# Interleaving projection pieces with transposes, and moving the context transposes last, in the attention stage of an eight-stage kernel

## The chip, the cores and the metric

The kernel runs on one core of a Trainium2 chip. The metric is the device time of one execution in microseconds; before the change the median of three executions is 2313.64 us (2311.55 to 2314.72).

## What is computed

The reference chains four attention layers and four feed-forward layers of different kinds on `x` (2 batches, 1024 rows, 256 features) with a context of 77 rows per batch. The change lies in the seventh link, called stage 6 in the kernel (stages count from 0), which is the last attention layer. Cut to what matters:

```
def _L3_xattn_ref(x, latents, mask, ...):      # x = context (77 rows), latents = layernormed rows (1024)
    xn = layer_norm(x, g_x, b_x)
    ln = layer_norm(latents, g_l, b_l)
    q = ln @ Wq
    kv_in = concatenate([xn, ln], axis=1)      # 77 + 1024 = 1101 keys
    k, v = split(kv_in @ Wkv)                  # 16 heads of 64
    sim = (q * 64 ** -0.5) @ k.T
    attn = softmax(where(mask, sim, max_neg))
    out = (attn @ v) @ Wout
    return layer_norm(out, g_o, b_o)
```

Everything is float32. Scores are computed with queries on the partitions, so that the softmax runs along the free axis; the probabilities must then be transposed before they can be multiplied with `v`.

## The kernel before

The program is written engine by engine: each engine has its own function `stage6` with its instructions in the order in which it will run them, and semaphores between them. Nothing is reordered by a scheduler.

**Units.** The 16 heads are taken in pairs, 8 pairs for each of 2 batches, so there are 16 pairs `n`, and a pair has 8 tiles of 128 queries. The loop runs over units `u`; in unit `u` TensorE (PE) computes the scores of tile `u = 8n + qt`, and transposes the probabilities of tile `u - 1`. There are 128 such tiles. In what follows the parts of a unit on PE are called

- *scores* (`scores`): the product with the context keys of both heads (2 x 77 columns), then with the 1024 other keys of each head, all from line 614, the helper for matmuls;
- *p0, p1, p2, p3* (`p_turn`, L1177): four transposes of 128 x 128 each; p0 and p1 are head 0 of the pair, p2 and p3 head 1. One group fills one PSUM bank;
- *c* (`ctx_turn`, L1184 and L1185): the two transposes of the 77 context keys;
- *r* (`sums_turn`, L1192): in even units, two transposes of the reciprocal sums of the softmax of a pair of tiles;
- *w0, w1* (`piece`): in even units, two pieces of the q, k and v projections for the next head pair. Which pieces come is set by `u % 8`: in 0 both halves of q (512 columns each), in 2 the first two blocks of v with the context keys, and 512 columns of k, in 4 and 6 shorter ones;
- *v* (`weigh`): in odd units, the product of the transposed probabilities of two tiles with v;
- *o* (`project`): the output projection, in units 60 to 66 and in those after 123, even ones only.

**The ring.** The results of p, c, r, w, v and o all go to a ring of three PSUM banks. `r6_no` numbers them in the order of the table, and

```
        def r6_bank(key):
            return 5 + r6_no[key] % 3
                def free_bank(key):
                    t = r6_no[key]
                    if t >= 3:
                        copied(pe, r6_keys[t - 3])
                    return r6_bank(key)
```

So before PE writes entry `t` it waits until entry `t - 3` has been copied out. ScalarE (ACT) copies p0 and p1 (L1727), w0 (L1696 for q; L1698, L1704 and L1705 for v and the context keys) and r (L1745). VectorE (DVE) copies w1 (L2401 for q, L2402 for k), c (L2482), p2 and p3 (L2485), and v (L2477, with the multiplication by the reciprocal sums).

**Softmax.** DVE finds the maxima of the two heads (L2463 over 1024 columns, L2464 joins the context's maximum and releases ACT). ACT then does the exponential of head 0 and of head 1 (L1738, 1101 columns each, followed by a read of the accumulated sum). On ACT a unit is: copy p0, copy p1, exponential of head 0, copy w0 (even units), exponential of head 1, copy r (even units). On DVE it is: the reciprocal sums (even units), the maxima, copy w1, or v in odd units, copy c, copy p2, copy p3.

The order in the table before is, for an even unit, p0, p1, w0, w1, c, p2, p3, r, and o where there is one; for an odd unit p0, p1, v, c, p2, p3.

Of the kernel before, what the change touches and what calls it, by code (L numbers as in the profile page):

```python
# [16 lines left out]
P = 128  # L17
# [6 lines left out]
C = 77  # L24
# [27 lines left out]
def build(nc, A, out, stages=ALL_STAGES):  # L52

    ctx = ExitStack()
    with ctx:
# [316 lines left out]
        NU = 128  # L372
        N7 = {77 + 4 * t: t for t in range(8)}
        r6_no, r6_sb, done = {}, {}, {"act": 0, "dve": 0}
        for u in range(NU + 5):
            even = u % 2 == 0
            turn = 1 <= u <= NU
            batch = [("p", u - 1, 0), ("p", u - 1, 1)] if turn else []
            if even and u // 8 < 15:
                batch += [("w", u // 8 + 1, u % 8), ("w", u // 8 + 1, u % 8 + 1)]  # L380
            if not even and 3 <= u < NU + 3:
                batch += [("v", (u - 3) // 2)]
            batch += [("c", u - 1), ("p", u - 1, 2), ("p", u - 1, 3)] if turn else []
            if even and 2 <= u <= NU:
                batch += [("r", (u - 2) // 2)]
            if even and u >= 4 and (u // 2 - 2) % 32 >= 28:
                batch += [("o", u // 2 - 2)]
            if u in N7:
                batch += [("n", N7[u])]
            for key in batch:  # L390
                act_copies = key[0] == "r" or key[0] == "p" and key[2] < 2 or key[0] == "w" and key[2] % 2 == 0
                eng = "act" if act_copies else "dve"
                done[eng] += 1
                r6_no[key] = len(r6_no)
                r6_sb[key] = (r6_act if act_copies else r6_dve, done[eng])
# [216 lines left out]
        def _(pe):  # L612
# [506 lines left out]
            def stage6():  # L1119
# [75 lines left out]
                def weigh(g):  # L1195

                    n = g // 4
                    copied(pe, ("p", 2 * g + 1, 1))
                    copied(pe, ("p", 2 * g + 1, 3))
                    bank = free_bank(("v", g))  # L1200
                    for i in range(NKT):
                        rows = P if i < NKT - 1 else C
                        for h in range(2):
                            r = 64 * h
                            last = mm(PS[r:r + 64, bank, 0:2 * P], s6_v[n % 2][0:rows, i, r:r + 64], s6_pt[g % 2][h][0:rows, i], start=(i == 0), stop=(i == NKT - 1))
                    last.then_inc(r6_mm, 1)
# [13 lines left out]
                for u in range(NU + 5):  # L1220
# [4 lines left out]
                    if u == 0:  # L1225
                        pe.wait_ge(ln_xa, 8 * half_no[6] + 8)
                        turn6(2, 0, 5)
                        turn6(3, 0, 6)
                        turn6(2, 1, 7)
                        pe.wait_ge(ln_fa, 4 * tr + 3)  # L1230
                        turn6(3, 1, 5)
                        pe.wait_ge(ln_fa, 4 * tr + 4)
                        pe.wait_ge(ln_fv, 4 * tr + 4)
                    if 1 <= u <= NU:
                        p_turn(u - 1, 0)
                        p_turn(u - 1, 1)
# [138 lines left out]
        def _(act):  # L1375
# [309 lines left out]
            def stage6():  # L1685
# [27 lines left out]
                for j in range(0, 8, 2):  # L1713
# [2 lines left out]
                            act.activation(XN[:, t, :], X[:, t, :], ACT.Identity, bias=ln_bias[:, t:t + 1], scale=lnrs[:, t:t + 1]).then_inc(ln_xa, 1)  # L1716
                    act.wait_ge(c6_mm, j + 1)
                    piece(0, j, j).then_inc(c6_sb, 1)
                for u in range(NU + 5):
                    even = u % 2 == 0  # L1720
                    n, j = u // 8 + 1, u % 8
                    if 1 <= u <= NU:
                        v = u - 1
                        g, c0 = v // 2, (v % 2) * P
                        for i in range(2):
                            bank = filled(("p", v, i))
                            act.activation(s6_pt[g % 2][0][:, 4 * i:4 * i + 4, c0:c0 + P], PS[:, bank, :].rearrange("p (a n) -> p a n", a=4), ACT.Copy).then_inc(r6_act, 1)  # L1727
                    if u < NU:
                        g = u // 2
                        if u == 0:  # L1730
# [5 lines left out]
                        for h in range(2):  # L1736
# [2 lines left out]
                                           accum_out=s6_sm[:, g % 2, 2 * (u % 2) + h:2 * (u % 2) + h + 1]).then_inc(a6_p, 1)  # L1739
                            if h == 0 and even and n < 16:  # L1740
                                piece(n, j, filled(("w", n, j))).then_inc(r6_act, 1)
                    if even and 2 <= u <= NU:
                        g = (u - 2) // 2
                        bank = filled(("r", g))
                        act.activation(s6_r[g % 2], PS[:, bank, 0:2 * P], ACT.Copy).then_inc(r6_act, 1)  # L1745
# [106 lines left out]
        def _(dve):  # L1852
# [533 lines left out]
            def stage6():  # L2386
# [17 lines left out]
                def filled(key):  # L2404

                    dve.wait_ge(r6_mm, r6_no[key] + 1)
                    return r6_bank(key)

                def normed(g):

                    t = 8 * (g // 32) + 2 * (g % 4)
# [34 lines left out]
                for u in range(NU + 6):  # L2446
# [31 lines left out]
                    if 1 <= u <= NU:  # L2478
                        v = u - 1
                        g, c0 = v // 2, (v % 2) * P  # L2480
                        bank = filled(("c", v))
                        dve.tensor_copy(s6_ptc[g % 2][:, :, c0:c0 + P], PS[0:C, bank, 0:2 * P].rearrange("p (h n) -> p h n", h=2)).then_inc(r6_dve, 1)  # L2482
                        for i in (2, 3):
                            bank = filled(("p", v, i))
                            dve.tensor_copy(s6_pt[g % 2][1][:, 4 * (i - 2):4 * (i - 2) + 4, c0:c0 + P], PS[:, bank, :].rearrange("p (a n) -> p a n", a=4)).then_inc(r6_dve, 1)  # L2485
                    if even and u >= 4 and (u // 2 - 2) % 32 >= 28:
                        normed(u // 2 - 2)
                    if u in N7:
# [170 lines left out]
```

## Time and profile before

| what | value |
|---|---|
| median of three executions | 2313.64 us (2311.55 to 2314.72) |
| the profiled execution | 2314.89 us |
| its span | 2313.1 us |
| PE busy | 2136.5 us, 92% of the span |
| DVE busy | 1397.3 us, 60% |
| ACT busy | 1027.7 us, 44% |
| stage 6 (first unit's scores to about the last transposes) | 1108 to 2196 us of the span, some 47% of it |

The profiled execution took 1.8 us more than its span, which begins with its first recorded instruction, and lies 1.25 us above the median. The busy time of PE is modelled from the starts of matmuls, which are pipelined: a transpose counts 0.27 us as busy, while in an undisturbed group one starts every 0.11 us. A short wait of PE therefore shows only partly as idle time, and is best read from the starts of neighbouring groups.

### The profile page before, as it was taken

The page shows a single profiled execution, that of the slowest core. Times are in us where ns is not written, and L with a number is a line of the kernel's source. Part 1 is how long each engine was busy: PE and PEld are TensorE (multiplying, and loading weights), DVE is VectorE, ACT ScalarE, POOL GpSimd, SP SyncE. Part 2 cuts the span into 40 slices and gives each one's busy share as a digit, 9 for nine tenths or more (in the row PEclk, how much of TensorE's full clock was granted, in tenths as well). Part 3 has the DMA queues.
Part 4 walks back from the last instruction along what each step waited for, and adds up shares of the span by engine and source line. Part 5 has one row for each costly group of instructions (what it writes and reads, how often), then busy time and mean ns, then how long its engine had stood idle before and what let it go on. Part 6 is the DMA issues. An engine that isn't in the chain of part 4 may idle for free.

```text
span 2313.1 us, 34544 instructions
## 1 busy us (share of the span) xinstructions
PE 2136.5 (92%) x13157; PEld 1517.1 (66%) x13157; DVE 1397.3 (60%) x3066; ACT 1027.7 (44%) x2143; POOL 129.4 (6%) x122
## 2 busy tenths in 40 slices
PE   6996997868999799796999999999999999999998
PEld 4874996434999678555566666666666666666653
DVE  5763112672444678687566666666666767677555
ACT  5652442530121522487445444454445444454445
POOL 1002111005122000000100000000000000000000
PEclk9997999889999999898999999999999999999999
DMA  3605897024797600200000000000000000000001
GB/s 116 175 3 169 306 328 237 19 77 135 258 324 267 199 1 1 78 1 7 5 1 1 1 1 1 1 1 1 1 1 1 1 1 1 1 1 1 1 1 37
DMA packets 109263, 159.78 MB, mean 69 GB/s; under 512 B 12555, under 2 KB 85165, under 8 KB 109101
## 3 DMA queue, kind: packets, MB, share of 16 engines
q1 hardware_dynamic: 101805, 134.80, 17.6%
q0 software_dynamic: 7296, 22.78, 2.9%
q8 instruction: 107, 1.75, 0.3%
q14 instruction: 55, 0.45, 0.1%
HBM read 127.64 MB, written 29.91 MB: 68 GB/s over the span
## 4 chain that ended last, share of the span: by engine, by line
PE 51%; DVE 4%; ACT 2%; issue 1%; ACTq 0%; DVEq 0%
PE ps L614 38%; PE ps L1177 10%; PE ps L1184 1%; ACT w_odd L1738 1%; PE ps L1192 1%; DVE small L2463 1%; PE ps L1080 0%; DVE arena L2485 0%; DVE arena L2402 0%; PE ps L1185 0%; DVE w_odd L2401 0%; DVE small L2348 0%; ACT xn_tok L1599 0%; PE ps L1089 0%; ACT out_feat L1656 0%
## 5 line engine op out<-in xcount | busy, mean ns | idle before, releaser
L614 PE MATMUL ps<-arena,w_odd 128*128 128x128 f32 (+4 forms) x2352 | 436.9, 439 | 3.0 <-DVE arena L2140 1.2
L614 PE MATMUL ps<-arena 128*64 128x256 f32 (+4 forms) x3216 | 388.4, 371 | 8.1 <-DVE arena L2271 4.3
L2463 DVE TENSOR_REDUCE small<-ps 128x1 f32<-128x1024 f32 x256 | 312.6, 1221 | 81.7 <-PE ps L614 81.5
L1727 ACT ACTIVATE arena<-ps 128x512 f32<-128x512 f32 x256 | 139.2, 595 | 452.0 <-PE ps L1177 451.9
L614 PEld LDWEIGHTS ps<-arena 128*64 128x64 f32 (+4 forms) x3216 | 254.2, 154 | 120.1 <-issue 22.4
L614 PEld LDWEIGHTS ps<-arena,w_odd 128*128 128x128 f32 (+3 forms) x2352 | 245.2, 187 | 105.1 <-issue 99.8
L1738 ACT ACTIVATE w_odd<-ps,small 128x1101 f32<-128x1101 f32 x256 | 302.8, 1183 | 9.7 <-DVE small L2464 7.3
L1177 PEld LDWEIGHTS ps<-ident,w_odd 128*128 128x128 f32 x2048 | 223.1, 141 | 123.4 <-issue 110.4
L1177 PE MATMUL ps<-ident,w_odd 128*128 128x128 f32 x2048 | 281.3, 277 | 12.0 <-DVE w_odd L2401 2.9
L2485 DVE COPY arena<-ps 128x512 f32<-128x512 f32 x256 | 164.3, 683 | 5.4 <-PE ps L1177 3.1
L614 PE MATMUL ps<-xn_feat,w_even 128*128 128x512 f32 (+1 forms) x352 | 137.9, 523 | 5.1 <-DVE xn_feat L2384 2.3
L1528 ACT ACTIVATE arena<-ps,arena 128x128 f32<-128x128 f32 x184 | 67.5, 368 | 92.9 <-PE ps L614 82.2
L614 PE MATMUL ps<-arena,w_even 128*128 128x256 f32 (+2 forms) x608 | 107.8, 330 | 0.5 <-DVE x_res L1921 0.5
L614 PE MATMUL ps<-xn_feat,w_odd 128*128 128x512 f32 x224 | 103.4, 602 | 0.0
L614 PE MATMUL ps<-w_odd,arena 128*128 128x256 f32 (+1 forms) x436 | 101.5, 379 | 0.0
L614 PEld LDWEIGHTS ps<-arena,w_even 128*128 128x128 f32 x608 | 94.8, 192 | 8.6 <-DVE x_res L1921 0.6
L614 PE MATMUL ps<-w_even,xn_feat 128*128 128x128 f32 (+1 forms) x576 | 96.2, 313 | 0.0
L1548 ACT ACTIVATE arena<-ps 128x128 f32<-128x128 f32 (+1 forms) x117 | 32.4, 277 | 141.2 <-PE ps L614 140.6
L614 PEld LDWEIGHTS ps<-xn_feat,w_even 128*128 128x128 f32 x352 | 62.2, 192 | 45.1 <-issue 38.9
L2161 DVE TENSOR_SCALAR arena<-ps,arena 128x256 f32<-128x256 f32 x62 | 30.0, 484 | 96.8 <-PE ps L614 96.8
L614 PEld LDWEIGHTS ps<-w_odd,arena 128*128 128x128 f32 (+1 forms) x436 | 79.5, 190 | 9.0
L614 PEld LDWEIGHTS ps<-w_even,xn_feat 128*128 128x128 f32 x576 | 73.7, 192 | 17.1 <-issue 16.8
(395 smaller groups left out, 2930.8 us busy)
## 6 DMA issues: line engine op xcount, KB each, us to landing
w_odd<-in_s_w SPq DMA_DIRECT2D x32, 1024.0 KB
w_odd<-in_s_wgu SPq DMA_DIRECT2D x30, 704.0 KB
w_even<-in_s_w SPq DMA_DIRECT2D x15, 1024.0 KB
arena<-expert_rows_in SPq DMA_DIRECT2D x62, 130.0 KB
w_odd<-in_s_wd SPq DMA_DIRECT2D x30, 256.0 KB
out_feat<-in_s_wgu SPq DMA_DIRECT2D x10, 704.0 KB, 4.2
expert_rows_in<-zero_row POOLq DMA_DIRECT2D x1, 5070.0 KB, 32.4
vo_rows<-w_odd SPq DMA_DIRECT2D x8, 616.0 KB
```

The costliest lines, as they stand in the source:

```text
L614: return pe.matmul(o, lhsT, rhs, start=start, stop=stop, **kw)
L1177: last = pe.transpose(PS[:, bank, j * P:(j + 1) * P], src[:, c0:c0 + P], ident[:, :])
L1184: pe.transpose(PS[0:C, bank, 0:P], s6_p[u % 2][0][:, S:KV], ident[:, :])
L1192: last = pe.transpose(PS[:, bank, i * P:(i + 1) * P], s6_rb[g % 2][:, 2 * i:2 * i + 2].rearrange("p h d -> p (h d)"), ident[:, :])
L1528: act.activation(s1_h[q][:, m], PS[:, (M * i + m) % 4, 0:TS], ACT.Gelu, bias=s1_bt[w][:, m:m + 1]).then_inc(per["mu_act", 1], 1)
L1548: act.activation(s3_s[0:rows, u % 2, 0:TS], PS[0:rows, u % 4, 0:TS], ACT.Silu).then_inc(per["mu_act", 3], 1)
L1727: act.activation(s6_pt[g % 2][0][:, 4 * i:4 * i + 4, c0:c0 + P], PS[:, bank, :].rearrange("p (a n) -> p a n", a=4), ACT.Copy).then_inc(r6_ ...
L1738: act.activation(s6_p[u % 2][h][:, 0:KV], s6_sc[h], ACT.Exp, bias=s6_nm[:, u % 2, h:h + 1], accum_out=s6_sm[:, g % 2, 2 * (u % 2) + h:2 * ...
L2161: dve.tensor_scalar(mx_y[st][v % 2][:, j], PS[:, 4 + n % 2, 0:D], es_xg[:, v, 1:2], None, ALU.mult).then_inc(per["md_sb", st], 1)
L2463: link(dve.tensor_reduce(m, s6_main[h], AX.X, ALU.max, negate=True))
L2485: dve.tensor_copy(s6_pt[g % 2][1][:, 4 * (i - 2):4 * (i - 2) + 4, c0:c0 + P], PS[:, bank, :].rearrange("p (a n) -> p a n", a=4)).then_inc( ...
```

## The change

In units `u` with `1 <= u < 120` and `u % 8` of 0 or 2 (29 units, called *long* here) the ring's order becomes p0, w0, p1, w1, r, p2, p3, c, then o. PE follows this order. ACT copies p1 no longer before the exponential of head 0 but after the copy of w0, that is ahead of the exponential of head 1. DVE copies c after p3. All other units stay as they are. `weigh` gets one more wait, for the copy of c, since that is no longer implied by the copy of p3.

```
+        def long_pieces(u):
+
+            return 1 <= u < 120 and u % 8 in (0, 2)
+
         for u in range(NU + 5):
             even = u % 2 == 0
             turn = 1 <= u <= NU
+            if long_pieces(u):
+                pieces = [("w", u // 8 + 1, u % 8 + i) for i in range(2)]
+                batch = [("p", u - 1, 0), pieces[0], ("p", u - 1, 1), pieces[1], ("r", (u - 2) // 2)]
+                batch += [("p", u - 1, 2), ("p", u - 1, 3), ("c", u - 1)]
+                if u >= 4 and (u // 2 - 2) % 32 >= 28:
+                    batch += [("o", u // 2 - 2)]
...
                     copied(pe, ("p", 2 * g + 1, 1))
                     copied(pe, ("p", 2 * g + 1, 3))
+                    copied(pe, ("c", 2 * g + 1))
...
+                    if long_pieces(u):
+                        p_turn(u - 1, 0)
+                        piece(n, j, free_bank(("w", n, j))).then_inc(r6_mm, 1)
+                        p_turn(u - 1, 1)
+                        piece(n, j + 1, free_bank(("w", n, j + 1))).then_inc(r6_mm, 1)
+                        sums_turn((u - 2) // 2)
+                        p_turn(u - 1, 2)
+                        p_turn(u - 1, 3)
+                        ctx_turn(u - 1)
+                        if u >= 4 and (u // 2 - 2) % 32 >= 28:
+                            project(u // 2 - 2)
+                        continue
...
-                        for i in range(2):
-                            bank = filled(("p", v, i))
-                            act.activation(s6_pt[g % 2][0][:, 4 * i:4 * i + 4, c0:c0 + P], PS[:, bank, :].rearrange("p (a n) -> p a n", a=4), ACT.Copy).then_inc(r6_act, 1)
+                        for i in range(1 if long_pieces(u) else 2):
+                            p_copy(v, i)
...
                             if h == 0 and even and n < 16:
                                 piece(n, j, filled(("w", n, j))).then_inc(r6_act, 1)
+                            if h == 0 and long_pieces(u):
+                                p_copy(u - 1, 1)
...
-                        bank = filled(("c", v))
-                        dve.tensor_copy(s6_ptc[g % 2][:, :, c0:c0 + P], PS[0:C, bank, 0:2 * P].rearrange("p (h n) -> p h n", h=2)).then_inc(r6_dve, 1)
+                        if not long_pieces(u):
+                            context_copy(v)
                         for i in (2, 3):
                             bank = filled(("p", v, i))
                             dve.tensor_copy(s6_pt[g % 2][1][:, 4 * (i - 2):4 * (i - 2) + 4, c0:c0 + P], PS[:, bank, :].rearrange("p (a n) -> p a n", a=4)).then_inc(r6_dve, 1)
+                        if long_pieces(u):
+                            context_copy(v)
```

**PE, a unit with `u % 8 == 2`, from piece w1 to the unit's end, before.** L614 is w1 (`w_even` holds the k weights here), L1184 and L1185 are c, L1177 first p2, then p3 (`w_odd` holds the probabilities), L1192 is r. `r6_act` and `r6_dve` are the waits for copies by ACT and by DVE.

```order
L614 MATMUL ps<-xn_feat,w_even 128x512 [waits r6_act]
L614 MATMUL ps<-xn_feat,w_even 128x512
L1184 MATMUL ps<-ident,w_odd 77x128 [waits r6_act,a6_p]
L1185 MATMUL ps<-ident,w_odd 77x128
L1177 MATMUL ps<-ident,w_odd 128x128 [waits r6_act,a6_p]
L1177 MATMUL ps<-ident,w_odd 128x128 x3
L1177 MATMUL ps<-ident,w_odd 128x128 [waits r6_dve,a6_p]
L1177 MATMUL ps<-ident,w_odd 128x128 x3
L1192 MATMUL ps<-ident,arena 128x128 [waits r6_dve,a6_rb]
L1192 MATMUL ps<-ident,arena 128x128
```

The same stretch after the change; 18 lines were added ahead of it, so that L632, L1195, L1202, L1203 and L1210 are what L614, L1177, L1184, L1185 and L1192 were.

```order
L632 MATMUL ps<-xn_feat,w_even 128x512 [waits r6_act]
L632 MATMUL ps<-xn_feat,w_even 128x512
L1210 MATMUL ps<-ident,arena 128x128 [waits r6_act,a6_rb]
L1210 MATMUL ps<-ident,arena 128x128
L1195 MATMUL ps<-ident,w_odd 128x128 [waits r6_act,a6_p]
L1195 MATMUL ps<-ident,w_odd 128x128 x3
L1195 MATMUL ps<-ident,w_odd 128x128 [waits r6_dve,a6_p]
L1195 MATMUL ps<-ident,w_odd 128x128 x3
L1202 MATMUL ps<-ident,w_odd 77x128 [waits r6_act,a6_p]
L1203 MATMUL ps<-ident,w_odd 77x128
```

Between w1 and p3 there are six transposes in both. r and c have changed places, and the last group of the unit now waits for ACT (the copy of r) where it waited for DVE (the copy of c).

**ACT, the same unit, before.** L1727 copies p0 and p1, L1738 is an exponential, L1698, L1704 and L1705 copy w0, L1745 copies r.

```order
L1727 ACTIVATE arena<-ps 128x4x128 [waits r6_mm] x2
L1738 ACTIVATE w_odd,small<-ps,small 128x1101 [waits a6_mx,r6_mm]
L1698 ACTIVATE arena<-ps 128x256 [waits r6_mm]
L1704 ACTIVATE w_even<-ps 64x77
L1705 ACTIVATE w_even<-ps 64x77
L1738 ACTIVATE w_odd,small<-ps,small 128x1101 [waits a6_mx]
L1745 ACTIVATE arena<-ps 128x256 [waits r6_mm]
```

The same unit after the change (L1754, L1773, L1729, L1735, L1736 and L1782 for L1727, L1738, L1698, L1704, L1705 and L1745):

```order
L1754 ACTIVATE arena<-ps 128x4x128 [waits r6_mm]
L1773 ACTIVATE w_odd,small<-ps,small 128x1101 [waits a6_mx,r6_mm]
L1729 ACTIVATE arena<-ps 128x256 [waits r6_mm]
L1735 ACTIVATE w_even<-ps 64x77
L1736 ACTIVATE w_even<-ps 64x77
L1754 ACTIVATE arena<-ps 128x4x128 [waits r6_mm]
L1773 ACTIVATE w_odd,small<-ps,small 128x1101 [waits a6_mx]
L1782 ACTIVATE arena<-ps 128x256 [waits r6_mm]
```

One copy of 128 x 512 has moved from ahead of the first exponential to ahead of the second, so that it stands between the first exponential and the copy of r.

## Rows read from the trace of the kernel before

**Rows 1.** The page: busy us, share of the span, instructions, by engine.

```profile
PE 2136.5 (92%) x13157; PEld 1517.1 (66%) x13157; DVE 1397.3 (60%) x3066; ACT 1027.7 (44%) x2143; POOL 129.4 (6%) x122
```

**Rows 2.** Windows of the span, us: busy time by engine, then PEclk, DMA share, GB/s.

```profile
1108.50:2195.00 1086.50, 1063.44 (x7094) 703.53 (x7095) 731.18 (x1498) 521.32 (x960) 2.98 (x1) 1.00 0.00 1
...
1127.10:1132.00 4.90, 4.90 (x18) 2.70 (x19) 2.59 (x8) 0.42 (x1) 0.00 (x0) 0.65 0.01 3
```

**Rows 3.** Waits in stage 6: us in total, times, longest us.

```profile
PE ps L1177 <- DVE w_odd L2401: 2.9, 13, 0.2
PE ps L1177 <- DVE arena L2402: 2.9, 13, 0.2
```

**Rows 4.** Timeline of unit 18, PE: start us, us, then [idle before].

```profile
1264.23 0.27 PE L1184 MATMUL ps<-ident,w_odd 128*77 128x128 f32 x1
...
1264.45 0.60 PE L1177 MATMUL ps<-ident,w_odd 128*128 128x128 f32 x4
1265.27 0.63 PE L1177 MATMUL ps<-ident,w_odd 128*128 128x128 f32 x4 [0.22 <-DVE arena L2402]
1265.73 0.38 PE L1192 MATMUL ps<-ident,arena 128*128 128x128 f32 x2
1265.95 0.43 PE L614 MATMUL ps<-w_even,w_odd 128*128 128x154 f32 x2
```

**Rows 5.** Timeline of unit 18, DVE.

```profile
1261.62 0.16 DVE L2464 TENSOR_TENSOR small<-small 128x1 f32<-128x1 f32 x1
...
1264.43 0.69 DVE L2402 COPY arena<-ps 128x512 f32<-128x512 f32 x1 [1.33 <-PE ps L614]
```

**Rows 6.** Timeline of unit 18, ACT.

```profile
1260.94 1.09 ACT L1727 ACTIVATE arena<-ps 128x512 f32<-128x512 f32 x2 [5.02 <-PE ps L1177]
1261.91 1.18 ACT L1738 ACTIVATE w_odd<-ps,small 128x1101 f32<-128x1101 f32 x1
...
1263.07 0.39 ACT L1698 ACTIVATE arena<-ps 128x256 f32<-128x256 f32 x1
...
1263.57 0.23 ACT L1705 ACTIVATE w_even<-ps 64x77 f32<-64x77 f32 x1
1263.82 1.18 ACT L1738 ACTIVATE w_odd<-ps,small 128x1101 f32<-128x1101 f32 x1
...
1266.15 0.39 ACT L1745 ACTIVATE arena<-ps 128x256 f32<-128x256 f32 x1 [1.06 <-PE ps L1192]
```

**Rows 7.** Timeline of unit 64, which also has a projection: DVE, ACT and PE.

```profile
1650.18 0.16 DVE L2464 TENSOR_TENSOR small<-small 128x1 f32<-128x1 f32 x1
...
1650.43 1.18 ACT L1738 ACTIVATE w_odd<-ps,small 128x1101 f32<-128x1101 f32 x1 [1.61 <-DVE small L2464]
...
1651.61 0.59 ACT L1696 ACTIVATE w_odd<-ps 128x512 f32<-128x512 f32 x1
...
1652.34 1.07 PE L1177 MATMUL ps<-ident,w_odd 128*128 128x128 f32 x8 [0.54 <-ACT w_odd L1696]
...
1653.84 1.97 PE L614 MATMUL ps<-w_even,xn_tok 128*128 128x256 f32 x8 [0.22 <-DVE arena L2485]
```

**Rows 8.** Timeline of unit 16, ACT and PE.

```profile
1245.06 1.19 ACT L1738 ACTIVATE w_odd<-ps,small 128x1101 f32<-128x1101 f32 x1
...
1246.73 1.18 ACT L1738 ACTIVATE w_odd<-ps,small 128x1101 f32<-128x1101 f32 x1
...
1249.26 0.38 PE L1192 MATMUL ps<-ident,arena 128*128 128x128 f32 x2
```

**Rows 9.** Timeline of unit 66: first exponential, and start of the projection.

```profile
1674.97 1.18 ACT L1738 ACTIVATE w_odd<-ps,small 128x1101 f32<-128x1101 f32 x1 [1.60 <-DVE small L2464]
...
1678.51 0.67 PE L614 MATMUL ps<-w_even,xn_tok 128*128 128x256 f32 x2 [0.22 <-DVE arena L2485]
```

**Rows 10.** Timeline of unit 74: first exponential, and start of the next unit.

```profile
1748.87 1.18 ACT L1738 ACTIVATE w_odd<-ps,small 128x1101 f32<-128x1101 f32 x1
...
1752.12 0.53 PE L614 MATMUL ps<-w_even,w_odd 128*128 128x154 f32 x2
```

More of the change, by code:

```diff
@@ L377, in build @@
             turn = 1 <= u <= NU
+            if long_pieces(u):
[4 more added lines that the diff above has]
+                    batch += [("o", u // 2 - 2)]
+                for key in batch:
+                    act_copies = key[0] == "r" or key[0] == "p" and key[2] < 2 or key[0] == "w" and key[2] % 2 == 0
+                    eng = "act" if act_copies else "dve"
+                    done[eng] += 1
+                    r6_no[key] = len(r6_no)
+                    r6_sb[key] = (r6_act if act_copies else r6_dve, done[eng])
+                continue
             batch = [("p", u - 1, 0), ("p", u - 1, 1)] if turn else []
@@ L1233, in stage6 @@
                         pe.wait_ge(ln_fv, 4 * tr + 4)
+                    if long_pieces(u):
[9 more added lines that the diff above has]
+                            project(u // 2 - 2)
+                        continue
                     if 1 <= u <= NU:
@@ L1718, in stage6, with p_copy @@
                     piece(0, j, j).then_inc(c6_sb, 1)
+                def p_copy(v, i):
+                    g, c0 = v // 2, (v % 2) * P
+                    bank = filled(("p", v, i))
+                    act.activation(s6_pt[g % 2][0][:, 4 * i:4 * i + 4, c0:c0 + P], PS[:, bank, :].rearrange("p (a n) -> p a n", a=4), ACT.Copy).then_inc(r6_act, 1)
                 for u in range(NU + 5):
@@ L1723, in stage6 @@
                         v = u - 1
-                        g, c0 = v // 2, (v % 2) * P
-                        for i in range(2):
-                            bank = filled(("p", v, i))
-                            act.activation(s6_pt[g % 2][0][:, 4 * i:4 * i + 4, c0:c0 + P], PS[:, bank, :].rearrange("p (a n) -> p a n", a=4), ACT.Copy).then_inc(r6_act, 1)
+                        for i in range(1 if long_pieces(u) else 2):
+                            p_copy(v, i)
                     if u < NU:
@@ L2407, in filled, with context_copy @@
                     return r6_bank(key)
+                def context_copy(v):
+                    g, c0 = v // 2, (v % 2) * P
+                    bank = filled(("c", v))
+                    dve.tensor_copy(s6_ptc[g % 2][:, :, c0:c0 + P], PS[0:C, bank, 0:2 * P].rearrange("p (h n) -> p h n", h=2)).then_inc(r6_dve, 1)
                 def normed(g):
```

## The prediction

> **What bounds the kernel now.** I read the page first. PE is busy for 2136.5 us of the span, DVE and ACT far less [rows 1]. The windows then give stage 6: 1063.44 of 1086.50 us PE-busy at a granted clock of 1.00 throughout [rows 2]. So PE sets the pace of the stage, and the change can only act through the moments at which PE waits inside a unit, or through waits that it adds. It adds and removes no arithmetic.
>
> The waits of PE in the stage show two groups that belong to the long units: transposes of L1177 wait 13 times for the copy of w1 by L2401 and 13 times for that by L2402 [rows 3]. The times look tiny, 2.9 us each, since a transpose's busy time is longer than its slot. The timeline shows the real size. In unit 18 (`u % 8` is 2) the group p2 starts at 1264.45 and p3 at 1265.27, 0.82 us later, while a slot is 0.11 us (the two of c fill 1264.23 to 1264.45) and four of them are 0.44 us [rows 4]. The wait is thus 0.38 us, and it ends with DVE's copy of w1, which runs from 1264.43 to 1265.12 [rows 5]. This wait, in 26 ordinary long units and in a different form in three others, is what a reordering of the ring could win: 26 x 0.38 = 9.9 us.
>
> **Part one: the wait ahead of p3.** Count the ring before: w0, w1, c, p2, p3; three entries ahead of p3 stands w1. After: w1, r, p2, p3; three ahead of p3 stands w1 again. Between the end of w1 on PE and the start of p3 lie two short transposes (c before, r after) and the four of p2, six slots either way: w1 ends where c starts, at 1264.23, and p3 could start at 1264.89 in both orders. What precedes w1 is the same work too (p0, p1, w0, in another order), so w1 ends at the same time, DVE starts its copy at the same time, and p3 waits for it until 1265.27 as before. Gain: 0. The move of p1 behind w0, and of c's copy behind those of p2 and p3 on DVE, does not touch this: c's copy stood behind w1's before as well.
>
> **Part two: the new wait of c.** Three entries ahead of c now stands r, and r is copied by ACT after the exponential of head 1. Before, r's neighbour waited for c's copy, which DVE had long made. So I follow ACT through unit 18:
>
> - First exponential. In the trace it starts at 1261.91, two copies after 1260.94, so a copy takes 0.485 us from start to start [rows 6]. With p1's copy moved away it waits only for DVE's maximum, ready at 1261.62 + 0.16 = 1261.78 [rows 5]. From such an end to an exponential that was waiting for it takes 0.09 us (1650.34 to 1650.43) [rows 7]. Start: 1261.87.
> - Copy of w0 starts 1.16 us later and holds ACT for 0.75 us (1263.07 to 1263.82) [rows 6]: 1263.03, and free at 1263.78.
> - Copy of p1, 0.485 us: the second exponential starts at 1264.27, where it started at 1263.82.
> - Copy of r: 1.16 us after it, 1265.43; it takes 0.39 us [rows 6], to 1265.82.
> - PE starts 0.14 us after the end of a copy by ACT (1651.61 + 0.59 = 1652.20, against 1652.34) [rows 7]: c can start at 1265.96.
>
> PE reaches c when p3 has been issued, at 1265.73, where r started before [rows 4]. It waits 0.23 us, and a group that restarts after a wait takes some 0.02 us more (p3: 0.46 for 0.44). The unit ends 0.25 us later. The odd unit behind it has no waits of the ring on PE in which this could be recovered: the stage is bound by PE, and a delay moves all that follows. Twelve units are of this kind (10, 18, ..., 114 but not 66 and 74): **+3.0 us**. Unit 2 runs its scores at the lower of the two clocks (0.65 in that window [rows 2]), so that the copies of p0 and p1 come late there, and moving one away frees the exponential; I count 0, at most 0.25.
>
> In units with `u % 8` of 0, w0 is a half of q: two exponentials are 1.67 us apart [rows 8], and w1 and w0 are both long on PE. From 1245.06: second exponential at 1245.06 + 1.67 + 0.485 = 1247.22, copy of r at 1248.38, its end at 1248.77, c free at 1248.91. PE gets there at 1249.26 [rows 8]. There are 0.35 us to spare: **0** for 13 units.
>
> Three long units have a late first exponential; there PE already waits for ACT's copy of w0 ahead of p2. After the change the row on ACT is w0, p1, exponential, r, and c waits at its end. From the first exponential to the start of c is 1.16 + 0.75 + 0.485 + 1.16 + 0.39 + 0.14 = 4.09 us, and 0.25 us for c itself. Unit 66: 1674.97 + 4.34 = 1679.31, where the projection started at 1678.51 [rows 9]: +0.80. Unit 74: 1748.87 + 4.34 = 1753.21 against 1752.12 [rows 10]: +1.09 at most, since its exponential may start a little earlier. Unit 64, with q for w0 (1.67 in place of 1.16 + 0.75): 1650.43 + 4.10 = 1654.53 against 1653.84 [rows 7]: +0.69. Together **+2.6 us**.
>
> **Part three, what costs nothing.** The second exponential ends 0.45 us later; the next unit's scores wait for it, but 1264.27 + 1.18 + 0.2 for the read of the sum is 1265.65, and those scores come at 1266.2. p1's copy now ends at 1264.38; p2, three entries behind, could start at 1264.45 and is held to 1264.52, which is hidden by p3's wait to 1265.27. r waits for w0's copy, done by 1263.8. `weigh` now waits for c's copy, which is DVE's third behind w1's (p2, p3, c); c is issued by 1266.2 and copied by about 1267, while `weigh` comes behind the next unit's scores and two groups, 3.2 us of work (4.9 x 0.65 [rows 2]). If that cover went, the product with v would be late. No DMA moves, and no instruction is added.
>
> **Sum.** 3.0 + 2.6 = +5.6 us on the profiled execution, 2314.89 to 2320.5. That execution lies 1.25 above the median, so the median goes from 2313.64 to **2319.2 us**, 0.24% slower.
>
> A rule to weigh against the rows: two copies take 0.485 us from start to start here [rows 6]. The Trainium skill (page "ScalarE: Activation LUTs", section "What ACT_TABLE_LOAD costs") gives 186 ns plus 0.833 ns per column for an activation with immediate operands, less 93 ns where two overlap; for 512 columns that is an estimate of 0.52 us, and the trace does not quite agree. By that page each of the 15 waits would be 0.035 us longer, and the sum 6.1 us.
>
> **Bounds of the unknown.** No row shows c waiting for r. From below it is 0 per unit, if ACT catches up; the three odd units alone then give +2.6. From above it is what the row of ACT gives if nothing overlaps: a copy at its full 0.60 us instead of 0.485, and both exponentials followed by their read, 1.39 instead of 1.16: 0.58 us more, 0.83 in all. I take 0.25, since every interval in it is one that ACT shows in this order of operations.
>
> **Rivals.** A change of 0.2% (4.6 us) is about what a measurement of this kernel can tell from none.
>
> - *ACT is in time.* Should PE come to c some 0.2 us later than I read, or ACT run ahead, the regular units cost nothing: 2313.64 + 2.6 = 2316.2. For it speaks that the margin is small; against it that the trace repeats its units to within hundredths.
> - *The wait ahead of p3 goes, and c doesn't wait.* If w1's copy did not decide (if, say, the release of p3 hung on ACT's copy of w0 or on the order of DVE's copies), alternating pieces and groups would win the 0.38 us in 26 units: 2313.64 - 9.9 = 2303.7. It decides only if c's wait is absent too, for p3's relief alone would bring PE to c earlier, to stand there for ACT. Against it: rows 3 name the copies of w1 in just 26 cases, and the count of the ring leaves w1 where it was. That the change doesn't do what it is for belongs here: the ring after is a new order with the same distance.
> - *The late case for ACT.* The chain on ACT is 0.45 us longer than I think, and the units of the other kind, with 0.35 to spare, wait too: 12 x 0.70 + 13 x 0.10 + 2.6 + 3 x 0.45 = 13.7 us, 2327.3.
> - *The clock.* In the window from 1127.10, behind a wait of PE, the clock was 0.65 [rows 2]. Fifteen more short waits could lower it. The scores and first groups there took 4.9 us, at full clock 0.65 of it, 3.2 us; 15 x 1.7 = 25 us, 2339. Against it: 26 waits of 0.38 us leave it at 1.00 in rows 2. The Trainium skill ("TensorE: Matmul & The Clock Gate", section "A second HAM failure mode: psum-queue depth-cycling") tells of a kernel that cycled through PSUM banks with short idle times of PE and whose clock kept switching between its two levels; that rule speaks against a change that adds a wait to a ring, but the trace of this ring so far doesn't agree with it.
>
> **How the numbers follow.** Forecast 0.62; ACT in time 0.21; faster 0.06; late ACT 0.08; clock 0.03. Of the forecast's 0.62 I give 0.07 to ends under 4.6 us, as a sum of 5.6 with an error of 0.1 us per unit may have. Faster 0.06, within 0.28, slower 0.66. The range goes from 2315.0 (ACT in time, less 1 us for the spread of the runs) to 2324.0 (the regular wait at 0.6 instead of 0.25): it leaves out the faster case, the clock and most of the late case.
>
> **What would show it.** In the profile after, p3 still starts 0.82 us after p2 in long units; the copy of r starts before c and right behind the second exponential; c in units with `u % 8` of 2 is released by ACT, 0.2 to 0.3 us after p3's last slot; and in the waits of PE the context transposes (L1202, before L1184) appear as held by the copy of r (L1782, before L1745) 12 to 15 times. Units with `u % 8` of 0 keep their length. The prediction is wrong if p3 starts 0.44 us after p2, or if c follows p3 without a gap.

## The result and the profile after

| | before | after |
|---|---|---|
| median of five executions | 2313.64 us (2311.22 to 2316.34) | 2321.69 us (2320.03 to 2326.81) |
| profiled execution | 2314.89 us, span 2313.1 | 2320.03 us, span 2318.3 |

The ratio is 1.0041, with a 95% interval of 1.0029 to 1.0053: 6.7 to 12.3 us slower. The forecast was 5.6 us and a time of 2319.2 in a range of 2315.0 to 2324.0. The direction and the range were right, and the size came out too small. The profiled execution alone shows +5.1 us, but beside what the change does to the waits, two things of about equal size and opposite sign stand in the difference of these two profiles; the experiments below find both.

The page of the changed kernel. Its first line holds something that the prediction had denied: 64 instructions more than the 34544 of before.

```profile
span 2318.3 us, 34608 instructions
## 1 busy us (share of the span) xinstructions
PE 2139.7 (92%) x13157; PEld 1513.7 (65%) x13157; DVE 1401.5 (60%) x3066; ACT 1026.3 (44%) x2143; POOL 129.4 (6%) x122
```

Against [rows 1] nothing has changed in the work. Now the timeline of unit 18 after the change, which answers to [rows 4 to 6]. First the loads of weights (PEld), since they part p2 from p3: L1210 is r, L1195 p2 and then p3, L1202 and L1203 are c, L632 the scores of unit 19. The columns are start us, us, and in brackets the idle time before and what ended it.

```profile
1262.71 0.14 PEld L1210 LDWEIGHTS ps<-ident,arena 128*128 128x128 f32 x1 [0.17 <-issue]
1263.02 0.42 PEld L1195 LDWEIGHTS ps<-ident,w_odd 128*128 128x128 f32 x4 [0.17 <-issue]
1263.71 0.42 PEld L1195 LDWEIGHTS ps<-ident,w_odd 128*128 128x128 f32 x4 [0.28 <-issue]
1264.45 0.14 PEld L1202 LDWEIGHTS ps<-ident,w_odd 128*77 128x77 f32 x1 [0.32 <-ACT w_odd L1773]
```

The same on PE itself, where the two groups are merged in one row:

```profile
1262.71 0.38 PE L1210 MATMUL ps<-ident,arena 128*128 128x128 f32 x2
1263.05 1.32 PE L1195 MATMUL ps<-ident,w_odd 128*128 128x128 f32 x8
1264.48 0.30 PE L1202 MATMUL ps<-ident,w_odd 128*77 128x128 f32 x1
1264.62 0.27 PE L1203 MATMUL ps<-ident,w_odd 128*77 128x128 f32 x1
1264.73 0.43 PE L632 MATMUL ps<-w_even,w_odd 128*128 128x154 f32 x2
```

And ACT: L1773 are the two exponentials, L1729 to L1736 the copy of w0, L1754 that of p1, L1782 that of r.

```profile
1260.39 1.18 ACT L1773 ACTIVATE w_odd<-ps,small 128x1101 f32<-128x1101 f32 x1 [0.34 <-DVE small L2507]
...
1261.56 0.38 ACT L1729 ACTIVATE arena<-ps 128x256 f32<-128x256 f32 x1
...
1262.31 0.60 ACT L1754 ACTIVATE arena<-ps 128x512 f32<-128x512 f32 x1
1262.80 1.18 ACT L1773 ACTIVATE w_odd<-ps,small 128x1101 f32<-128x1101 f32 x1
...
1263.95 0.38 ACT L1782 ACTIVATE arena<-ps 128x256 f32<-128x256 f32 x1
```

The chain stands as forecast: 4.09 us from the first exponential (1260.39) to c (1264.48), with 1.17, 0.75, 0.49, 1.15, 0.38 and 0.15 for its steps. p3 still waits for w1's copy: from the end of w1, where r starts (1262.71), to p3 it is 1.0 us (1263.71 for its weights), as in [rows 4] from 1264.23 to 1265.27. Behind p3 PE now stands until r has been copied: p3's four transposes begin by 1264.10, one more slot of 0.11 us would be 1264.21, and c begins at 1264.48, 0.27 us later. The row of L1202 above names the second exponential (L1773) as what ended the wait, but that was done at 1263.98; the copy of r ended at 1264.33, and it is the only other one that c waits for. In unit 18 the wait is too short to show as idle time of PE. It does so in three units, and there the copy of r is named:

```profile
PE ps L1202 <- ACT arena L1782: 1.1, 3, 0.4
```

The clearest reading is the length of each unit, from the start of its scores to that of the next one's. Where the clock is the same it repeats to some 0.01 us. "Before, again" and "after, again" are second profiles, from the experiments; the first of them comes from another chip.

| unit | before | before, again | after | after, again |
|---|---|---|---|---|
| `u % 8` of 0 (median) | 8.36 | 8.36 | 8.37 | 8.36 |
| `u % 8` of 2 (median) | 7.99 | 7.99 | 8.25 | 8.25 |
| 2 | 9.72 | 8.09 | 8.35 | 8.35 |
| 64 | 16.05 | 16.04 | 16.64 | 16.64 |
| 66 | 16.18 | 16.18 | 16.91 | 16.91 |
| 74 | 8.62 | 8.61 | 9.53 | 9.53 |
| odd units (median) | 8.49 | 8.49 | 8.49 | 8.49 |

Against "before, again": 12 x 0.27 = 3.2, unit 2 0.27, units 64, 66 and 74 0.60 + 0.73 + 0.92 = 2.25. Together 5.7 us; I had 5.6. Two units are left out of this. Unit 75, behind unit 74, takes 8.49 us for 8.59, so 0.10 comes back. Unit 126 took 14.95 us in "before, again" and 16.3 to 16.5 in the other three profiles, behind a wait of 2.5 us that all have; the last section comes back to it. The sum of all units but 0 and 126 is 5.8 us.

### The profile page after: what moved, and what is told of

It is laid out like the page before. It is cut to its first block, busy times and chain, and to the rows that moved or that the text cites. A ratio compares the mean times of both kernels' runs of the same rounds, so it can differ in the third digit from the quotient of the medians.

```text
span 2318.3 us, 34608 instructions
## 1 busy us (share of the span) xinstructions
PE 2139.7 (92%) x13157; PEld 1513.7 (65%) x13157; DVE 1401.5 (60%) x3066; ACT 1026.3 (44%) x2143; POOL 129.4 (6%) x122
## 4 chain that ended last, share of the span: by engine, by line
PE 51%; DVE 4%; ACT 3%; issue 1%; ACTq 0%; DVEq 0%
PE ps L632 38%; PE ps L1195 10%; PE ps L1202 1%; ACT w_odd L1773 1%; DVE small L2506 1%; PE ps L1203 1%; PE ps L1210 0%; PE ps L1098 0%; DVE w_odd L2438 0%; DVE arena L2528 0%; DVE small L2385 0%; ACT out_feat L1687 0%; PE ps L1107 0%; ACT xn_tok L1630 0%; ACT arena L1754 0%
## 5 line engine op out<-in xcount | busy, mean ns | idle before, releaser
L632 PE MATMUL ps<-arena,w_odd 128*128 128x128 f32 (+4 forms) x2352 | 436.2, 438 | 3.0 <-DVE arena L2177 1.2
L632 PE MATMUL ps<-arena 128*64 128x256 f32 (+4 forms) x3216 | 388.2, 371 | 8.2 <-DVE arena L2308 4.4
L1754 ACT ACTIVATE arena<-ps 128x512 f32<-128x512 f32 x256 | 142.2, 595 | 482.4 <-PE ps L1195 482.0
L632 PEld LDWEIGHTS ps<-arena 128*64 128x64 f32 (+4 forms) x3216 | 254.4, 154 | 120.1 <-issue 22.6
L632 PEld LDWEIGHTS ps<-arena,w_odd 128*128 128x128 f32 (+3 forms) x2352 | 245.3, 187 | 105.1 <-issue 99.8
L1773 ACT ACTIVATE w_odd<-ps,small 128x1101 f32<-128x1101 f32 x256 | 302.8, 1183 | 19.0 <-DVE small L2507 17.2
L1195 PEld LDWEIGHTS ps<-ident,w_odd 128*128 128x128 f32 x2048 | 223.2, 141 | 128.4 <-issue 117.7
L1195 PE MATMUL ps<-ident,w_odd 128*128 128x128 f32 x2048 | 285.7, 277 | 8.1 <-DVE w_odd L2438 2.9
L632 PE MATMUL ps<-xn_feat,w_even 128*128 128x512 f32 (+1 forms) x352 | 139.8, 522 | 5.1 <-DVE xn_feat L2421 2.3
L632 PE MATMUL ps<-arena,w_even 128*128 128x256 f32 (+2 forms) x608 | 107.8, 330 | 0.5 <-DVE x_res L1958 0.5
L632 PE MATMUL ps<-xn_feat,w_odd 128*128 128x512 f32 x224 | 103.5, 603 | 0.0
L632 PE MATMUL ps<-w_odd,arena 128*128 128x256 f32 (+1 forms) x436 | 101.5, 379 | 0.0
L632 PEld LDWEIGHTS ps<-arena,w_even 128*128 128x128 f32 x608 | 94.7, 192 | 8.6 <-DVE x_res L1958 0.6
L632 PE MATMUL ps<-w_even,xn_feat 128*128 128x128 f32 (+1 forms) x576 | 96.3, 313 | 0.0
L632 PEld LDWEIGHTS ps<-xn_feat,w_even 128*128 128x128 f32 x352 | 61.0, 192 | 38.6 <-issue 32.5
L632 PEld LDWEIGHTS ps<-w_odd,arena 128*128 128x128 f32 (+1 forms) x436 | 79.5, 190 | 9.0
L632 PEld LDWEIGHTS ps<-w_even,xn_feat 128*128 128x128 f32 x576 | 73.7, 192 | 17.0 <-issue 16.7
```

The costliest lines, as they stand in the source:

```text
L632: return pe.matmul(o, lhsT, rhs, start=start, stop=stop, **kw)
L1195: last = pe.transpose(PS[:, bank, j * P:(j + 1) * P], src[:, c0:c0 + P], ident[:, :])
L1773: act.activation(s6_p[u % 2][h][:, 0:KV], s6_sc[h], ACT.Exp, bias=s6_nm[:, u % 2, h:h + 1], accum_out=s6_sm[:, g % 2, 2 * (u % 2) + h:2 * ...
```

## The experiments

Three chips served. On the first (both parts alone, c ahead of w1 in two kinds of units, the changed kernel again) the kernel before had a median of 2313.43 us (23 executions), on the second (half of the units, the extra wait alone, before again, three kinds with the extra wait) 2298.98 (31), on the third (the two runs without the extra wait) 2299.16 (11). The ratios are always to before on the same chip. Of the 18.0 us between the spans of the two profiles of before, 14.9 lie ahead of stage 6, 1.6 in unit 2 and 1.5 in unit 126; the other units are the same. The edits are shown against the changed kernel, if nothing else is said.

### One part alone: alternate

The order is p0, w0, p1, w1, c, p2, p3, r on PE and in the table, and c is copied on DVE where it was before; ACT is left as in the change.

```
-                batch = [("p", u - 1, 0), pieces[0], ("p", u - 1, 1), pieces[1], ("r", (u - 2) // 2)]
-                batch += [("p", u - 1, 2), ("p", u - 1, 3), ("c", u - 1)]
+                batch = [("p", u - 1, 0), pieces[0], ("p", u - 1, 1), pieces[1], ("c", u - 1), ("p", u - 1, 2), ("p", u - 1, 3), ("r", (u - 2) // 2)]
```

> One part of the change alone: pieces and groups alternate (p0, w0, p1, w1, c, p2, p3, r) with ACT's order as in the change, c stays where it was. Theory A (the loss is c waiting for the copy of r, which ACT makes behind the delayed second exponential): units with u % 8 of 2 come back to 7.98 us (8.25 in the changed kernel), since the last group r waits for DVE's copy of c again; only units 64, 66, 74 lose some 0.5 us each, about +1.5 us against before. Rival B (the later copy of p1 and second exponential cost time by themselves): those units stay near 8.25 and the kernel at about +5 us.

Measured: 2316.36 us, ratio 1.0012 (1.0003 to 1.0021). Units with `u % 8` of 2 take 7.94 us, 0.04 less than before; 64, 66 and 74 lose 0.49, 0.62 and 0.36. The sum is +0.9 us by the units. PE at the end of unit 18 (L1201 and L1202 are c, L1194 p2 and p3, L1209 r):

```profile
1266.55 0.27 PE L1201 MATMUL ps<-ident,w_odd 128*77 128x128 f32 x1
...
1266.89 1.33 PE L1194 MATMUL ps<-ident,w_odd 128*128 128x128 f32 x8
1268.05 0.38 PE L1209 MATMUL ps<-ident,arena 128*128 128x128 f32 x2
1268.27 0.30 PE L631 MATMUL ps<-w_even,w_odd 128*128 128x154 f32 x1
```

From w1's end (1266.55) to the unit's end (1268.27) it is 1.72 us, as before (1264.23 to 1265.95 in [rows 4]). The delayed second exponential costs nothing there by itself. Rival B falls.

### The other part alone: context transposes last

The order is p0, p1, w0, w1, r, p2, p3, c, with ACT's order of before the change.

```
+                batch = [("p", u - 1, 0), ("p", u - 1, 1), pieces[0], pieces[1], ("r", (u - 2) // 2), ("p", u - 1, 2), ("p", u - 1, 3), ("c", u - 1)]
...
-                        for i in range(1 if long_pieces(u) else 2):
+                        for i in range(2):
...
-                            if h == 0 and long_pieces(u):
-                                p_copy(u - 1, 1)
```

> The other part alone: p0, p1, w0, w1, r, p2, p3, c, with ACT's order as before the change (p0, p1, first exponential). Theory A: the copy of r ends 0.45 us sooner than in the change, at 5.4 us + 2.1 us = some 0.2 us before PE comes to c, so the regular units keep 7.98 and 8.36 us; units 64, 66, 74 lose 0.2, 0.3 and 0.6 us: about +1.1 us. Neither part alone makes the loss, both together do. Rival C (c behind r on the ring costs the 0.27 us whatever ACT's order): units with u % 8 of 2 at 8.25, +5 us. The wait of p3 for w1's copy stays at 0.38 us in both theories.

Measured: 2317.16 us, ratio 1.0016 (1.0007 to 1.0025). The units keep 7.99 and 8.36 us; 64, 66 and 74 lose 0.10, 0.24 and 0.61: +0.95 us by the units. ACT's copy of r, and PE from r to the unit's end:

```profile
1263.82 0.37 ACT L1779 ACTIVATE arena<-ps 128x256 f32<-128x256 f32 x1
```

```profile
1263.07 0.38 PE L1209 MATMUL ps<-ident,arena 128*128 128x128 f32 x2
1263.29 0.60 PE L1194 MATMUL ps<-ident,w_odd 128*128 128x128 f32 x4
1264.11 0.63 PE L1194 MATMUL ps<-ident,w_odd 128*128 128x128 f32 x4 [0.22 <-DVE arena L2436]
1264.57 0.27 PE L1201 MATMUL ps<-ident,w_odd 128*77 128x128 f32 x1
```

r is copied by 1264.19, and with the 0.15 us of release PE could have c at 1264.34; it comes there at 1264.57. So each part alone leaves the regular units where they were, and the 0.27 us need both: c behind r on the ring, and the copy of p1 ahead of r's on ACT. The p3 wait is untouched (1263.29 to 1264.11, the 0.82 us of before). Rival C falls.

### What would shorten the wait ahead of p3

If the wait is set by the distance from w1 to the entry that needs its bank, putting c ahead of w1 lengthens it from six slots to eight. ACT's order is that of before, and DVE copies c first.

```
+                batch = [("p", u - 1, 0), ("p", u - 1, 1), pieces[0], ("c", u - 1), pieces[1], ("p", u - 1, 2), ("p", u - 1, 3), ("r", (u - 2) // 2)]
...
+                    if long_pieces(u):
+                        context_copy(u - 1)
                     if even and n < 16:
                         piece(n, j + 1, filled(("w", n, j + 1))).then_inc(r6_dve, 1)
```

> A test of part one: long units in the order p0, p1, w0, c, w1, p2, p3, r, ACT's order as before, DVE copies c ahead of w1. Two full groups (eight slots) now lie between w1 and the entry that needs its bank, r, in place of six slots. Theory A: PE's wait for w1's copy falls from 0.38 to 1.04 - 0.87 = 0.17 us in 26 units: units of 8.36 become 8.14, of 7.98 become 7.77, the kernel 5.5 us faster than before (about 2308). Rival D (the wait is not set by the distance from w1 but by the release of DVE or ACT): no change of the units, 0 us.

Measured: 2308.71 us, ratio 0.9979 (0.9967 to 0.9991), 2.1 to 7.6 us faster. The units take 8.15 and 7.73 us.

```profile
1259.68 1.88 PE L631 MATMUL ps<-xn_feat,w_even 128*128 128x512 f32 x4
1261.40 1.04 PE L1194 MATMUL ps<-ident,w_odd 128*128 128x128 f32 x8
1262.43 0.41 PE L1209 MATMUL ps<-ident,arena 128*128 128x128 f32 x2
```

```profile
1261.60 0.69 DVE L2436 COPY arena<-ps 128x512 f32<-128x512 f32 x1 [1.17 <-PE ps L631]
```

p2 and p3 now run through, and r comes 1.03 us after w1's end, the time in which p3 was released before (1.04 us). (The eight slots of 0.11 us make 0.87 of it, and 0.16 is the wait that is left.) So the wait is what the release of w1's bank takes less the slots that lie between, and rival D falls. The order of DVE's copies, which this run changes too, has no part in it: DVE begins the copy of w1 0.20 us after w1's end in both orders (1264.43 after 1264.23 in [rows 4 and 5], 1261.60 after 1261.40 here) and is idle ahead of it. The count of the ring in part one was the right argument.

### The changed kernel again

> The changed kernel once more, on the chip of the other runs, for a second profile and as their yardstick. By the unit lengths it should be 5.2 to 5.6 us over before; the five runs so far gave +8. If +8 is the true value, something beside the long units costs 2 to 3 us and the second profile should show where; if it is the scatter of the moments at which the clock rises after pauses, the stretches outside the long units differ between the two profiles of the same kernel by 1 to 2 us, and not always in the same sense.

Measured: 2322.70 us, ratio 1.0040 (1.0026 to 1.0054). The units are those of the first profile (table above). The span is 2316.1, 2.2 us shorter than the first, all of it before stage 6, whose first scores start at 1105.58 instead of 1107.77. So much for scatter. But the median is again 9 us over before, and the intervals of both measurements begin at 6.0 us or more, above the 5.7 of the units. Something is missing from the account. The next four runs went after it.

### Half of the units

```
-            return 1 <= u < 120 and u % 8 in (0, 2)
+            return 1 <= u < 120 and u % 8 == 0
```

> The change in the units with u % 8 of 0 alone (14 of the 29). Theory A: 13 of them keep 8.36 us, since ACT has the copy of r done 0.35 us before PE needs its bank, and unit 64 takes 0.6 us longer: +0.6 us. If the kernel is nevertheless 2 us or more slower, as all changed kernels of the first four runs were 1 to 3 us above what their units add up to, something that all of them share costs time outside the long units.

Measured: 2302.35 us, ratio 1.0008 (0.9999 to 1.0017). Units of the kind 0 take 8.36 us, unit 64 takes 16.64 (+0.6), the others are as in the first profile of before, with unit 2 at 9.72 again. By medians it is 3.4 us over before, where the units give 0.6; the interval holds both.

### The extra wait alone

```
                     copied(pe, ("p", 2 * g + 1, 3))
+                    copied(pe, ("c", 2 * g + 1))
```

added to the kernel before, against which it is shown.

> The kernel before with one thing added: the product with v also waits for the copy of c (already implied by the copy of p3, so it never holds). The changed kernel has 64 instructions more than the one before, one in each odd unit. Theory A: 0 us, the units keep their lengths. Theory E: this instruction, or what it does to PE's queue, is the 1 to 3 us that all changed kernels share.

Measured: 2300.65 us, ratio 1.0006 (0.9997 to 1.0015). All units keep their lengths, and the profile counts 34608 instructions, as after the change. The time does not tell this from no change; the end of its profile, below, does.

### The kernel before again

> The kernel before under another label, for a second profile and as a test of the comparison itself: the ratio should hold 1. In the first profile unit 2 took 9.72 us at a lower clock, while the four other kernels show 7.8 to 8.4 there. Theory A: the second profile has unit 2 near 8.1 us and its other units unchanged to 0.01 us, which would put the first profile of before 1.6 us too high in this place.

Measured: 2301.39 us, ratio 1.0005 (0.9995 to 1.0014). The same code is 2.4 us above itself by medians, so differences of medians of 1 to 2 us are not to be read. Unit 2 took 8.09 us, with the clock at 1.00 where [rows 2] has 0.65:

```profile
1112.40:1117.30 4.90, 4.90 (x31) 3.44 (x32) 3.55 (x8) 1.84 (x3) 0.00 (x0) 1.00 0.01 3
```

So the first profile of before is 1.6 us too long in unit 2. The first scores of stage 6 came at 1108.37 there and at 1107.77 after the change. By the units the spans should then differ by 5.7 - 1.6 - 0.6 = 3.5 us; they differ by 5.2. The rest, 1.7 us, is at the very end. The waits of the queue that stores the output, first in the kernel before, then in the changed one (L55 is the end of the program):

```profile
SPq L55 <- DMA out_dram<-x_res: 2.6, 1, 2.6
```

```profile
SPq L55 <- DMA out_dram<-x_res: 4.3, 1, 4.3
```

And the transfers of the last 9 us of the span, before and after. The row GB/s has 40 slices of 0.225 us:

```profile
GB/s 0 0 0 0 0 0 0 0 0 0 0 0 0 0 0 0 0 0 0 278 350 355 337 350 355 287 18 0 14 314 341 346 360 341 355 255 5 0 0 0
DMA packets 1056, 1.05 MB, mean 117 GB/s; under 512 B 32, under 2 KB 1056, under 8 KB 1056
## 3 DMA queue, kind: packets, MB, share of 16 engines
q1 hardware_dynamic: 1056, 1.05, 34.9%
```

```profile
GB/s 0 0 0 0 0 0 0 0 0 0 0 123 350 337 355 360 341 355 110 0 0 164 414 332 328 337 337 305 50 9 9 23 23 23 27 23 0 0 0 0
DMA packets 1057, 1.07 MB, mean 118 GB/s; under 512 B 32, under 2 KB 1056, under 8 KB 1056
## 3 DMA queue, kind: packets, MB, share of 16 engines
q1 hardware_dynamic: 1056, 1.05, 34.7%
q8 instruction: 1, 0.02, 1.0%
```

In the changed kernel one packet of instructions, 16 KB, falls under the last transfer of the output. It took 1.39 us where an output packet takes 0.05, and the last packet of the output ended 5.47 us after PE's last matmul had started, instead of 3.80. Before, the last transfer keeps some 350 GB/s to its end. After, it drops to 9 and then 23 GB/s for its last 1.6 us, which is what packets of 1 KB make one after another (1 KB in 0.047 us is 22 GB/s). This fits one of the 16 DMA engines getting to its share of the output late, behind the packet of instructions; the trace doesn't name the engine of a packet. The kernel with the extra wait alone has the packet too, and ends at 4.93 us; the second profile of before has none, and ends at 3.80.

### The change without its extra wait

The wait for c's copy can go without a race: when PE writes v it has waited for the entry three ahead in the ring, which is c itself, or o, which DVE copies behind c.

```
-                    copied(pe, ("c", 2 * g + 1))
```

> The change without its added wait of the product with v for the copy of c; the ring gives it anyway, since c (or o behind it) stands three entries ahead of v. So 64 instructions of PE fewer, and the count of before. Theory F: the 64 instructions move the fetch of the last 16 KB of instructions under the last transfer of the output, which then lands 1.7 us later (4.2 us after the last transposes without, 5.9 with it); the profile of this kernel has no such fetch at the end, the last output lands at 4.2 us, the units are those of the changed kernel (8.25, and 9.5, 16.6, 16.9 us for units 74, 64, 66), and the kernel is 5.8 us over before, not 7.5. Rival: the late landing belongs to the order of the units or to chance, and stays at 5.9 us.

Measured: 2306.30 us, ratio 1.0033 (1.0021 to 1.0046), 4.8 to 10.6 us over before. The units are those of the changed kernel (8.25; 16.64, 16.91 and 9.53). The profile has 34544 instructions, no packet of instructions at the end, and

```profile
SPq L55 <- DMA out_dram<-x_res: 2.6, 1, 2.6
```

The interval of the time holds both 5.8 and 7.5, so the 1.7 us rest on the profiles: all eight profiles of kernels with the extra wait (the changed one twice, both parts alone, half of the units, c ahead of w1 in two and in three kinds, the extra wait alone) have the packet and end 0.9 to 2.0 us late (0.9 and 1.1 in the two where it falls under the transfer before the last one); the four without it (before twice, this one, and the last of the next section) do not.

### The better order, in three kinds of units

The order p0, p1, w0, c, w1, p2, p3, r, as in the run with c ahead of w1, in units with `u % 8` of 0, 2 and 4, first with the extra wait, then without it.

```
+            return 1 <= u < 120 and u % 8 in (0, 2, 4)
```

> The order p0, p1, w0, c, w1, p2, p3, r of the previous run, now also in units with u % 8 of 4 (15 more). There p3 waits 0.12 us for w1's copy in the kernel before. Theory A: two groups between w1 and r are longer than the copy of the shorter w1, so that wait goes: 7.31 becomes 7.17 us, the kernel 2 us faster than with two kinds, about 7.5 us under before. Rival: c's copy, now ahead of w1's on DVE, comes late behind the second maximum and holds p3, and nothing is gained in these units.

> The order p0, p1, w0, c, w1, p2, p3, r in units with u % 8 of 0, 2 and 4, without the added wait. Theory F: the units of the run with three kinds (8.15, 7.73, 7.17) and the end of before (last output 4.2 us after the last transposes): 2.8 + 3.1 + 2.0 + 0.2 (unit 2) = 8.1 us under before. Rival: as with the added wait, some 7 us under.

Measured: 2292.89 us, ratio 0.9970 (0.9956 to 0.9983), and 2292.02 us, ratio 0.9967 (0.9955 to 0.9979). The units take 8.15, 7.73 and 7.17 us in both. The last is the best kernel of this study: 2299.16 to 2292.02 on the same chip, 4.8 to 10.3 us faster than before, 7.9 by the units (13 x 0.21, 12 x 0.26, 0.26 for unit 2, 13 x 0.14; units 60 and 68 of the third kind wait elsewhere and kept their length). So the copy of c ahead of w1's holds up nothing there, and the first run's rival falls. The time can't tell theory F from the second run's rival, since the interval holds both 8 and 7 us; the profile can: the last output ends 3.80 us after PE's last matmul has started, as before, and 5.11 us in the run with the extra wait. Unit 20 of it, where PE runs from the k piece on without a gap:

```profile
1263.26 1.03 PE L631 MATMUL ps<-xn_feat,w_even 128*128 128x256 f32 x4
1264.13 1.04 PE L1194 MATMUL ps<-ident,w_odd 128*128 128x128 f32 x8
1265.00 0.38 PE L1209 MATMUL ps<-ident,arena 128*128 128x128 f32 x2
```

## Why the prediction was right, and where it fell short

**Part one held.** p3 waits for w1's copy as long as before, and the run with c ahead of w1 showed the reason, the number of slots between. One detail was off: I expected p3 to start 0.82 us after p2; it is 0.69, since p2 itself waited 0.12 us for p1's copy, where I had 0.07. Both end in the same moment, w1's copy, so it cost nothing.

**Part two held in mechanism and size.** 4.09 us from the first exponential to c, as summed; 0.27 us per regular unit with `u % 8` of 2, for 0.25; 0.60, 0.73 and 0.92 in units 64, 66 and 74, for 0.69, 0.80 and "at most 1.09". In unit 74 the exponential started a little earlier, as allowed for. Unit 2 was counted 0 and costs 0.27. The units with q pieces are free, as forecast. One sign that I had named came out otherwise: in the waits of PE the context transposes stand for the copy of r only 3 times, not 12 to 15, because most of a wait of 0.27 us hides behind the 0.27 us that the last transpose of p3 counts as busy; in the waits of the weight loads they stand 15 times. "A delay moves all that follows" has one exception, unit 75 with its 0.10 us. What I had not seen is that two edits share the cause: either by itself leaves the regular units as they were, or 0.04 us shorter, and costs about 1 us in all, lost in units 64, 66 and 74.

**Part three failed in one sentence:** "no instruction is added". The added wait in `weigh` is a semaphore wait of its own in each of 64 odd units. It never holds PE, and the odd units kept their 8.49 us. But with it one more packet of instructions is fetched (107 of them on that queue before, 108 after, 107 again without the wait), and this one lands under the last output: +1.7 us. The sum had no term for it. 5.7 + 1.7 = 7.4 us lie in the intervals of both comparisons (6.7 to 12.3, and 6.0 to 12.5); 5.7 lies in neither. What is left between 7.4 and the medians' 8.1 and 9.3 us is no more than the 2.4 us by which before differs from itself.

The other runs bear this out. By the units alone the run with the context transposes last, at 0.95 us, lies outside its interval too (1.6 to 5.8). With the late end of its own profile added to its units, every kernel lies inside: 2.9 and 1.9 us for the two parts alone, 2.6 for half of the units, 1.1 for the extra wait alone, -4.3 for c ahead of w1, -6.6 for the same in three kinds. Most medians still lie above these sums, by up to 1.9 us, and no run shows why.

That the time fell within the range has some luck in it. The upper end, 2324.0, was put there for a longer wait of c, not for a cost at the end of the kernel.

**The rivals.** c does wait for ACT, so "ACT is in time" fell; p3's wait did not go; ACT's chain was not late; and the clock stayed at 1.00 over the long units. The rule of the Trainium skill on PSUM banks and the clock ("TensorE: Matmul & The Clock Gate", section "A second HAM failure mode: psum-queue depth-cycling") is not borne out by this trace: 15 more short waits in the ring left the clock where it was, at 1.00 from 1108.5 to 2200.2 us. For ScalarE the measured 0.49 us from the start of a copy to what follows it agrees with [rows 6] and not with the estimate of 0.52 us worked out from the Trainium skill ("ScalarE: Activation LUTs", section "What ACT_TABLE_LOAD costs").

## What to carry to other kernels

In a ring of buffers the wait of an entry is set by what lies between it and the entry whose buffer it takes, and by who copies that one: count both for each entry, before and after, and follow the copying engine's own queue to the end of the unit. Two harmless reorderings can meet in one chain. A wait that is implied already is still an instruction, and in this kernel 64 of them brought a fetch of instructions to where nothing covers it, the end.

## What was not expected of the hardware

- One packet of 16 KB of instructions took 1.0 to 1.8 us among the packets of an output transfer that take 0.05 us each, and with it the end of the kernel came 0.9 to 2.0 us later.
- The clock fell after some long waits of PE and not after others in the same place of the same code: unit 2, after a wait of 1.7 us, ran at 0.65 in one profile of before and at 1.00 in the other (9.72 and 8.09 us); among all twelve profiles it did so twice. Unit 126, after a wait of 2.5 us, took 14.95 us in two profiles, at 1.00, and 16.2 to 16.6 in the other ten; in the first profile of before the clock there was 0.86 to 0.88. In one run unit 62, where PE always waits some 1.9 us for ACT, was followed by matmuls at the lower clock, 17.67 us for 15.99. The windows of that stretch, first before, then in the run with c ahead of w1:

```profile
1624.50:1635.50 11.00, 9.06 (x50) 7.78 (x49) 4.57 (x9) 4.53 (x8) 0.00 (x0) 1.00 0.00 0
```

```profile
1619.00:1630.00 11.00, 9.06 (x42) 7.45 (x41) 4.47 (x8) 4.52 (x8) 0.00 (x0) 0.84 0.00 0
```

Each such case is worth 1.3 to 1.7 us. The executions of one kernel differ by 4 to 9 us, and the stretch ahead of stage 6, which no edit touches, took 1105.58 to 1112.28 us in the six profiles with spans of 2308 to 2319 us, so that such cases there may make most of it; that is not shown.
